# A recurrent kernel's index digits made in the small cell, and the first tokens sent apart

## What is computed

```python
m_from = lstm_last(base_emb[from_seq], seq_Wx, seq_Wh, seq_b)      # 64 steps, hidden 64
m_to = lstm_last(base_emb[to_seq], seq_Wx, seq_Wh, seq_b)
x = concatenate([num_emb[f][numbers], freq_emb[f][freqs]])          # 11 features, 32 steps
nwf = lstm_last(x, nwf_Wx[f], nwf_Wh[f], nwf_b[f])                  # hidden 8, tables of 1000 rows
y = relu(concatenate([goby, bools, m_from, m_to, counts, nwf]) @ reduce_W + reduce_b)
```

## Time and profile before

| what | before |
|---|---|
| median of 3 runs | 1712.02 us (1709.75 to 1712.13) |
| the profiled execution, its own time | 1714.94 us |
| its span, first to last instruction | 1713.1 us |
| busy share of the span | PE 94%, DVE 88%, ACT 77%, POOL 56% |
| mean granted TensorE clock | 0.989 |
| share of the chain that ended last | PE 53%, DVE 17%, ACT 15%, issue 9%, POOL 2% |
| DMA | 444.19 MB, mean 259 GB/s |

### The profile page before, as it was taken

One profiled execution on the slowest core, in us unless ns is written; L12 is line 12 of the kernel. 1 busy time (PEld: TensorE's weight loads), 2 busy tenths in 40 slices (PEclk: granted clock), 3 DMA queues, 4 the chain that ended last, 5 costly groups with the idle time before them and its releaser, 6 DMA issues.

```text
span 1713.1 us, 57020 instructions
## 1 busy us (share of the span) xinstructions
PE 1610.2 (94%) x23780; PEld 619.1 (36%) x23780; DVE 1509.0 (88%) x1573; ACT 1314.0 (77%) x2011; POOL 955.3 (56%) x473
## 2 busy tenths in 40 slices
PE   3799999999999999999999999999999999999997
PEld 0233333333333333333333333333333333333334
DVE  6788988989988989988989988988988988988984
ACT  4577777877777877777877778877778877778874
POOL 1445666776666776666754444554444554444553
PEclk8899999999999999999999999999999999999999
DMA  8678789898889898889788789899889888788870
GB/s 285 223 253 261 248 263 276 264 276 271 256 268 284 250 284 260 270 264 284 251 287 262 260 263 277 260 275 267 273 265 280 256 277 274 256 267 273 248 241 24
DMA packets 165793, 444.19 MB, mean 259 GB/s; under 512 B 45728, under 2 KB 103584, under 8 KB 132640
## 3 DMA queue, kind: packets, MB, share of 16 engines
q1 hardware_dynamic: 162112, 439.63, 81.8%
q0 software_dynamic: 2560, 0.15, 0.6%
q10 hardware_dynamic: 864, 0.75, 0.1%
HBM read 423.42 MB, written 6.82 MB: 251 GB/s over the span
## 4 chain that ended last, share of the span: by engine, by line
PE 53%; DVE 17%; ACT 15%; issue 9%; POOL 2%; DVEq 0%; POOLq 0%; ACTq 0%
PE e_ps L479 16%; PE ab L619 11%; PE f_ps L619 9%; PE ab L511 7%; DVE kept L493 7%; ACT gate L673 5%; DVE f_ps L705 5%; DVE seq_c L710 4%; ACT f_ps L671 3%; PE ab L425 3%; ACT tanh_c L664 3%; PE ab L560 2%; POOL ig L697 2%; ACT f_ps L673 2%; PE ab L570 2%
## 5 line engine op out<-in xcount | busy, mean ns | idle before, releaser
L697 POOL TENSOR_TENSOR ig<-gate 128x1024 f32<-128x1024 f32 x192 | 411.9, 2145 | 696.3 <-ACT seq_x L432 293.7
L479 PE MATMUL e_ps<-hot,tab 128*32 128x512 bf16 x8448 | 527.5, 384 | 61.6 <-DVE kept L493 56.8
L493 DVE SCALAR_TENSOR_TENSOR kept<-high,cst,e_ps 128x1024 f32<-128x1024 uint8 x352 | 449.1, 1276 | 49.6 <-PE e_ps L479 43.8
L619 PE MATMUL ab<-seq_h,seq_wh 64*64 64x512 f32 x3024 | 401.2, 590 | 0.0
L479 PEld LDWEIGHTS e_ps<-hot,tab 128*32 128x32 bf16 x8448 | 214.0, 97 | 486.8 <-issue 342.7
L469 DVE TENSOR_SCALAR hot<-low,cst 128x4096 bf16<-128x4096 bf16 x256 | 320.6, 1281 | 13.2 <-PE e_ps L479 13.2
L731 POOL TENSOR_TENSOR seq_h<-gate,tanh_c 128x1024 f32<-128x1024 f32 x128 | 308.9, 2414 | 31.8 <-ACT tanh_c L664 31.6
L673 ACT ACTIVATE gate<-ab,nwf_bias 128x512 f32<-128x512 f32 (+2 forms) x384 | 188.4, 553 | 166.2 <-PE ab L570 103.0
L671 ACT ACTIVATE gate<-ab 128x1024 f32<-128x1024 f32 x256 | 262.5, 1026 | 17.6 <-PE ab L619 8.8
L664 ACT ACTIVATE tanh_c<-seq_c 64x512 f32<-64x512 f32 (+1 forms) x384 | 241.9, 630 | 29.8 <-POOL nwf_h L731 22.1
L664 ACT ACTIVATE gate<-ab 64x512 f32<-64x512 f32 (+1 forms) x384 | 228.5, 595 | 9.4
(11 more groups left out here) (99 smaller groups left out, 1809.1 us busy)
## 6 DMA issues: line engine op xcount, KB each, us to landing
low<-low_digits SPq DMA_DIRECT2D x256, 1024.0 KB
low<-low_bytes SPq DMA_DIRECT2D x96, 512.0 KB
tok<-seq_tokens SPq DMA_DIRECT2D x128, 384.0 KB
high<-high_digits SPq DMA_DIRECT2D x1408, 32.0 KB
nwf_hq<-nwf_h SPq DMA_DIRECT2D x62, 128.0 KB
raw<-in_indices SPq DMA_DIRECT2D x32, 176.0 KB
low_digits<-low_of SPq DMA_DIRECT2D x32, 88.0 KB, 3.2
nwf_hq<-nwf_h SPq DMA_DIRECT2D x62, 32.0 KB, 3.0
```

Of the source, the lines that this page charges most:

```text
L479: last = nc.tensor.matmul(e_ps[32 * g:32 * g + 32, i, :], tab[:, part, 2 * m + ty, :], hot[:, p % HOT_RING, g, i, :], start=(part == 0), s ...
L493: nc.vector.scalar_tensor_tensor(out=kept[:, p % KEPT_RING, :, :], in0=wanted, scalar=cst[:, C_HIGH:C_HIGH + 1], in1=e_ps[:, :, :], op0=AL ...
L619: last = nc.tensor.matmul(flat(bank)[to:to + 64, cols], lhs(rows, half, block), rhs(rows, block, a, b), start=start, stop=stop)
L697: nc.gpsimd.tensor_tensor(ig[:, cols], gates[0][:, n % 2, cols], gates[1][:, n % 2, cols], ALU.mult).then_inc(ig_ready, 1)
```

## The change

Three things are moved. (1) The digits of round r from 3 are made in the small cell `nwf(r-3,1)`, those of round 1 in cell 1 and of round 2 in cell 4, each behind all of that cell's compares and keeps and just ahead of `scale_c`; POOL's ig of that cell waits for them. (2) The tokens of the first two steps (four rows, 128x64) come as an input of their own, are made right behind the digits of round 0 and stored to a DRAM tensor of their own; `make_tokens` on all tokens stands behind the tables, and SP's store of them behind the loads of token rows 2 and 3. Token row 4, and ACT's last gate of cell 0 (which overwrites the tile that holds the tokens), wait for that store. (3) The raw indices of round 1 are loaded behind pair 3.

```diff
+FIRST_NWF = NUMBER["nwf", 0, 0]
-ROUND_AT = {(0, 3)[_r - 1] if _r < 3 else NUMBER["nwf", _r - 2, 0]: _r for _r in range(FIRST_ROUNDS, NWF_T)}
+ROUND_AT = {(1, FIRST_NWF)[_r - 1] if _r < 3 else NUMBER["nwf", _r - 3, 1]: _r for _r in range(FIRST_ROUNDS, NWF_T)}
+FIRST_TOKENS = 4
...
+        def make_first_tokens(dve):
+            dve.wait_ge(s_first, 16)
+            in_range(dve, first_near[:, :], first_raw[:, :].bitcast(I16)[:, 0:first_near.shape[1]], first_raw[:, :], VOCAB,
+                     first_near[:, :].bitcast(BF16)).then_inc(first_made, 1)
...
             if s == 0:
+                sp.wait_ge(first_stored, 16)
+            elif s == FIRST_TOKENS:
                 sp.wait_ge(tokens_stored, 16)
...
+            if n == 0 and g == 3:
+                act.wait_ge(tokens_stored, 16)
...
                 load_raw(sp, 0)
-                sp.dma_start(tok_raw, tokens).then_inc(s_tokens, 16)
-                load_raw(sp, 1)
+                sp.dma_start(first_raw[:, :], first_tokens).then_inc(s_first, 16)
+                sp.dma_start(tok_raw[:, :], tokens).then_inc(s_tokens, 16)
                 store_digits(sp, 0)
...
                 make_digits(dve, 0)
-                make_tokens(dve)
+                make_first_tokens(dve)
                 make_x_weights(dve)
                 make_tables(dve)
+                make_tokens(dve)
...
-                    if n in ROUND_AT and CELLS[n][0] == "seq":
-                        make_digits(dve, ROUND_AT[n])
...
                     for p in compared[:2]:
                         compare_pair(dve, p)
-                        if p == compared[0] and n in ROUND_AT and CELLS[n][0] == "nwf":
-
-                            make_digits(dve, ROUND_AT[n])
                     for p in pairs[1:]:
                         keep_wanted(dve, p)
                     for p in compared[2:]:
                         compare_pair(dve, p)
+                    if n in ROUND_AT:
+                        make_digits(dve, ROUND_AT[n])
...
+                    if n in ROUND_AT:
+                        pool.wait_ge(digits_made, ROUND_AT[n] + 1)
                     input_product(pool, n)
```

More of the change, by code:

```diff
@@ L103 @@
 LAST = NCELLS - 1
-FIRST_NWF = NUMBER["nwf", 0, 0]
 LAST_SEQ = NUMBER["seq", SEQ_T - 1, 1]
@@ L134, in at_least, with build @@
         eng.wait_ge(sem, value)
-def build(nc, few, tokens, indices, goby_emb, bool_emb, count_emb, tables, seq_x_w, seq_h_w, rows, bias, rest_rows,
+def build(nc, few, first_tokens, tokens, indices, goby_emb, bool_emb, count_emb, tables, seq_x_w, seq_h_w, rows, bias, rest_rows,
           seq_rows, dense_rows, consts, out):
@@ L149, in build @@
         byte_dram = nc.dram_tensor("low_bytes", [NWF_T, NPAIRS, 4 * CH * 2], U8, kind="Internal").ap()
+        first_dram = nc.dram_tensor("first_digits", [FIRST_TOKENS, 4 * CH], BF16, kind="Internal").ap()
         tok_dram = nc.dram_tensor("seq_tokens", [SEQ_T, SLOTS // 2, 2, 2, LANES], BF16, kind="Internal").ap()
@@ L211, in build @@
         tok_of = gates[3][:, 0, :].bitcast(BF16)
+        first_raw = sb("first_raw", [P, FIRST_TOKENS * W // P], I32)
+        first_near = sb("first_near", [P, FIRST_TOKENS * W // P], I16)
         spare = kept[:, :, :, :].rearrange("p a b c -> p (a b c)")
@@ L248, in build @@
         s_tokens = sem("s_tokens")
+        s_first = sem("s_first")
         s_cst = sem("s_cst")
@@ L258, in build @@
         s_small_set = sem("s_small_set")
+        first_made = sem("first_made")
+        first_stored = sem("first_stored")
         tokens_made = sem("tokens_made")
@@ L404, in load_tokens @@
             if s == 0:
+                sp.wait_ge(first_stored, 16)
+            elif s == FIRST_TOKENS:
                 sp.wait_ge(tokens_stored, 16)
[L406 to L408 removed]
+            if s < FIRST_TOKENS:
+                of = first_dram[s:s + 1, :]
+            else:
+                of = tok_dram[step:step + 1, 4 * k:4 * k + 4, :, :, :].rearrange("t h z o l -> t (h z o l)")
+            sp.dma_start(tok[:, s % 2, :], of.to_broadcast([TOK_ROWS, 4 * CH])).then_inc(tok_here[s % 2], 16)
         def seq_compare(dve, s):
@@ L826, in _ @@
                     load_pair(sp, p)
+                load_raw(sp, 1)
+                for s in range(2, FIRST_TOKENS):
+                    load_tokens(sp, s)
+                sp.wait_ge(tokens_made, 1)
+                sp.dma_start(tok_dram.rearrange("t (k h) z o l -> (t k) (h z o l)", k=2),
+                             tok_of).then_inc(tokens_stored, 16)
                 sp.dma_start(few_in[:, :, :], few).then_inc(s_few, 16)
                 load_raw(sp, 2)
-                for s in range(2, 2 + AHEAD):
-                    load_tokens(sp, s)
                 for dst, src in ((rest_w[:, :], rest_rows), (seq_out_w[:, :], seq_rows)):
@@ L1089, in laid_out @@
     dense_rows = np.tile(w[146:234].reshape(FEATURES, NWF_H, OUT).transpose(1, 0, 2), (SLOTS, 1, 1))
-    return [few.reshape(5, P, SLOTS).transpose(1, 0, 2), tokens, indices, f["L0_rec_goby_emb"], f["L0_rec_bool_emb"],
+    first_tokens = tokens[:FIRST_TOKENS].reshape(P, -1)
+    return [few.reshape(5, P, SLOTS).transpose(1, 0, 2), first_tokens, tokens, indices, f["L0_rec_goby_emb"], f["L0_rec_bool_emb"],
             f["L0_rec_count_emb"], tables, seq_x_w.reshape(P, 4 * SEQ_H), seq_h_w, rows, bias, rest_rows.reshape(P, OUT), w[8:136],
             dense_rows.reshape(P, FEATURES * OUT),            constants()]
-_NAMES = ["few", "tokens", "indices", "goby_emb", "bool_emb", "count_emb", "tables", "seq_x_w", "seq_h_w", "rows",
+_NAMES = ["few", "first_tokens", "tokens", "indices", "goby_emb", "bool_emb", "count_emb", "tables", "seq_x_w", "seq_h_w", "rows",
           "bias", "rest_rows", "seq_rows", "dense_rows", "consts"]
```

6 lines of the change are left out of this document (3 added, 3 removed).

## The result

| | kernel before | with the change |
|---|---|---|
| median of the runs on one chip | 1710.88 us (4 runs, 1709.21 to 1712.13) | 1726.24 us (4 runs, 1724.49 to 1727.27) |
| ratio to before | | 1.0089 (1.0072 to 1.0107) |
| profiled execution: its own time, its span | 1714.94, 1713.1 us | 1727.27, 1725.5 us |
| the same kernel once more, on another chip | 1713.66 us (9 runs) | 1732.21 us (4 runs), ratio 1.0108 (1.0092 to 1.0123) |

The change makes the kernel slower by 15.4 us, 0.9%. The sign of the forecast was right, its size was not: 1715.5 us was said, and the range ended at 1721.5.

What follows compares the result with a forecast made beforehand. The loop of DVE and POOL was taken to set the pace, the DMA engines at the start. Start -4.7, round 1 -2.8, small cells +20.3, large cells -9.3 gave +3.5 us: 1715.5 us from 1712.0, range 1705 to 1721.5.

Steps and rivals of the forecast that it cites:

- Small cell, +0.70 us: Small cells with digits: late ig delays add_c and the next token compare meets POOL's h; 29 x 0.70 = +20.3 us.
- Large cells of rounds 15 to 29, -0.62: Large cells without gather: removing digits gains 0.62 us each until ACT is late; 15 x 0.62 = -9.3 us.
- Large cells of rounds 2 to 14: 0: Large cells with gathers: scale_c already waits for ACT, which hides the whole digit pass, so removing it gains 0.
- gather rounds gain too: Rival: PE's 0.7 us lateness goes or stops mattering; rounds 2 to 14 gain 0.62 us each, -8.1, 1707.4 us; chance 0.08.
- the list of what stands behind the late ig on POOL: Small cell, worked out on cell 97: h of cell 96 follows ig and meets the next token compare; 0.70 us.
- The rival of 0.9 us a cell: Small cells cost 0.9 us, by the whole overlap or pushed gathers; +5.8, 1721.3 us, slower; chance 0.15.
- the start, -4.7 us together with rounds 1 and 2: Cells 0 to 5: loads go out and land 3.4 us earlier, digits leave cells 0 and 3; -4.7 us (0 to -8).
- The rival with a chance of 0.12: The start gives nothing: loads land when DVE asks, no sooner; 1720.2 us, slower; chance 0.12.
- the 4.1 us: Cell 3: its digits go, 1.99 us stretched to about 4.1 by an instruction that took 2.34 us.
- 1.1 was counted: PE's look-up in cell 3 after a shorter wait: 1.48 instead of 2.75 us possible; 1.1 us taken as regained.
- Round 1's large cell, -2.8: Cell 10: digits stand on DVE's path with ten small-table instructions; 2.0 plus 0.8 from a faster look-up, -2.8 us.
- the rule for the token compare: Exclusive DVE/POOL port lock: the small-cell compare would stand still all 0.55 us, total some 6 us higher.

Runs made afterwards that it cites:

- run 11: Kernel before with the first five of seven digit instructions of rounds 18 to 31 in the small cell, the last two in the large one; 1702.24 us, ratio 0.9942.
- run 1: Kernel before with only the digits of rounds 3 to 31 moved to the small cells, POOL's ig waiting; start and rounds 1 and 2 as before; 1729.76 us, ratio 1.0100.
- run 4: Changed kernel with the 80 gathers in seq and large cells only, none in small cells; 1724.14 us, ratio to before 1.0064.
- run 5: The changed kernel itself, unaltered, measured once more; 1732.21 us, ratio to before 1.0108.
- run 2: Kernel before with only the start changed (first tokens an input apart), all digits in their old cells; 1712.05 us beside 1712.60, ratio 0.9996.
- run 3: Kernel before with only the digits of rounds 1 and 2 moved, to cells 1 and 4, POOL's ig waiting for them; 1714.95 us, ratio 1.0013.
- the control: The repeat of the unaltered changed kernel, the same as run 5; 1732.21 us, ratio to before 1.0108.
- run 7: Kernel before with digits of rounds 3 to 31 in small cells and the 80 gathers in seq cells only, four a round; 1723.32 us, ratio 1.0052.
- run 6: Changed kernel without POOL's wait for the digits in small cells, the wait kept in cells 1 and 4; 1805.14 us, ratio to before 1.0534.
- run 9: Kernel before with two digit instructions of rounds 18 to 31 in small cells, and ten small-table instructions moved from cell 10 to 7; 1705.57 us, ratio 0.9959.

## Why the prediction was right in sign and wrong in size

- **Small cell, +0.70 us: right.** Every link came as written, within 0.1 us. In rounds without gathers it measured 0.62 (cell 97 and 98 took 8.06 and 7.60 us instead of 8.01 and 7.12, the next 8.28 instead of 8.20); the 0.08 too much is part of the slack that run 11 found.
- **Large cells of rounds 15 to 29, -0.62: right.** 10.90 instead of 11.34, and 8.05 instead of 8.23 behind it. Small and large cancel, and rounds 16 to 29 stay at 51.4 us; +1.2 us was said for them together.
- **"Large cells of rounds 2 to 14: 0"** held with PE late (runs 1, 4, 5). In the first trace of the change PE was in time and they took 0.70 less: the rival "gather rounds gain too", by a difference between executions that the change has no part in.
- **The step that failed first** is the list of what stands behind the late ig on POOL. It had h of cell 96 and stopped there, since it was worked out on cell 97, a cell without a gather, and taken for all 29. In 14 of them a gather stands behind h. Run 4 takes it away and 0.74 us a round go with it: about +10 us that the sum did not hold. The rival of 0.9 us a cell, "by the whole overlap or since gathers are pushed too", named it and gave it 0.2 us.
- **The step that failed second** is the start, -4.7 us together with rounds 1 and 2. That row 2 goes out 3.4 us earlier and so lands 3.4 us earlier is false: token rows went out 1.6 us earlier, and DVE took row 2 at 29.7 to 32.5 us with the old start and at 29.9 to 31.3 with the new one. The rival with a chance of 0.12 held (run 2, -0.5 us). And in cell 3 I took the standstill away with the digits, while the compares took their place (4.56 us), so that 2.1 of the 4.1 us stayed; nor did the look-up there get faster (2.75 us), for which 1.1 was counted. Runs 2 and 3 make it +1.8, so 6.5 us.
- **Round 1's large cell, -2.8: right.** In run 1 the digits' 2.0 us went from cell 10 (11.40 instead of 13.40), and with what the faster look-up gave behind it cells 10 to 13 took 36.77 us instead of 39.76, so 3.0 less.

With the two failed steps put right the sum is 3.5 + 10 + 6.5 = 20 us, beside 18.5 in the control, whose trace has PE late as the profile before has (1732.21 against 1713.66). The measured parts add up as well: run 1 has +17.2, runs 2 and 3 have +1.8. That they come so close is in part luck, as the start is known to 2 us only.

The first result is 15.4, not 18.5. The two traces of the change explain it in part: with PE in time the cells behind cell 10 take 7.8 us less (the control's span is 6.1 us longer, though it reached cell 10 1.7 us earlier), and the medians, 1726.24 and 1732.21, differ by 6.0. The medians of the kernel before differ by 2.8 the same way, which leaves about 3 of it. Why those differ stays open, as does why PE is late: not its own cell's gather (run 7), not the kernel (run 5).

## What to carry to other kernels

A gap on one engine is not free time while another engine's long operation runs beside it: before filling it, list everything that the neighbour does from its next release on, in each kind of round, not in the one that is easiest to read. Moving work pays as far as the slack of both places reaches, so move the part that fits: two or five of the seven instructions gave 0.62 us a round, all seven gave nothing. Work issued 1.6 us earlier into full DMA engines landed no earlier here: look for the limit before counting on an earlier issue.

## What the runs showed of the hardware

- **DVE and POOL.** An int16 pass over 352 columns took 0.25 us alone and 2.30 in run 6, an f32 sum over 16 columns 0.18 and 2.28 in run 9: the wait goes by what is left of POOL's product, not by the size of the DVE instruction. It is not always DVE that stands still: in cell 2 of the kernel before, compares ran from 52.96 to 56.10 us at their full pace, and h, which started beside them at 53.21, took 5.11 us instead of 2.37. Keeps and `scale_c`, one operand of which is in PSUM, kept their 1.27 and 1.22 us beside POOL. The Trainium skill, SBUF — State Buffer, section "SBUF: two separate sides", has both: a DVE instruction in a two-port performance mode or with two SBUF inputs contends with GpSimd for the shared port pair, an exclusive lock. The trace agrees, with a standstill of DVE 0.14 to 0.2 us shorter than the overlap.
- **Gathers stretch too.** One gather on POOL took 0.98 us alone, 2.34 before and 3.65 in the change, ending 0.85 us behind the last compare. The same section of the Trainium skill warns of it: descriptors of a DMA issued on GpSimd are not written while a DVE instruction in a two-port performance mode runs. The trace agrees in kind, the longest gather being the one that stood beside two whole pair compares. The prediction named the rule for the token compare and did not work it out for the gather.
- **PE in rounds with gathers** is 0.7 us late in the large cell in some traces and in time in others, two of one and the same kernel included (run 5).
